# A graph layer with attention, linear mixing and a mixture of experts: the mixing product moved beside the edge gathers, the node stage unrolled, expert choice and placing rearranged

## The reference, cut to what matters

```python
xn = layernorm(x)
# graph attention, 4 heads of 64
h = (xn @ W).reshape(n, 4, 64)
logits = leaky_relu(a_src[src] + a_dst[dst], 0.2)
alpha = softmax of logits over the edges of one dst
gnn = relu(segment_sum(alpha * h[src], dst) + bias)
# linear attention, 4 heads of 32: one context matrix for all nodes
k = softmax(xn @ W_k, over the nodes);  context = k^T v;  mix = (q*scale) @ context @ W_out + b_out
x = x + gnn + mix
# mixture of experts, 8 experts, the best 2 of each node
xf = layernorm(x);  gate = xf @ Wg + bg;  top 2, softmax over the two
x = x + sum_e w_e * (gelu(xf @ W1[e] + b1[e]) @ W2[e] + b2[e])
```

## Time and profile before

| what | us |
|---|---|
| median of 3 runs | 1132.69 |
| lowest, highest | 1130.98, 1139.04 |
| the profiled execution | 1128.08 |
| its span | 1126.2 |
| TensorE busy | 935.8 (83%) |
| DVE busy | 514.0 (46%) |
| ACT busy | 364.9 (32%) |
| POOL busy | 596.7 (53%) |

### The profile page before, as it was taken

One profiled execution on the slowest core, in us unless ns is written; L12 is line 12 of the kernel. 1 busy time (PEld: TensorE's weight loads), 2 busy tenths in 40 slices (PEclk: granted clock), 3 DMA queues, 4 the chain that ended last, 5 costly groups with the idle time before them and its releaser, 6 DMA issues. The chain is left out here.

```text
span 1126.2 us, 19443 instructions
## 1 busy us (share of the span) xinstructions
PE 935.8 (83%) x5146; PEld 809.9 (72%) x5147; DVE 514.0 (46%) x1398; ACT 364.9 (32%) x1055; POOL 596.7 (53%) x591
## 2 busy tenths in 40 slices
PE   4999878878777687787864955699999999999995
PEld 3897656657566575665743845699999999899994
DVE  5488665665665656656646767111111111111110
ACT  4754332323323323333211310233333333333331
POOL 2477777777777777777739006233333333333331
PEclk9998787786878868778686867899999999999998
DMA  6356655555555555555684310466655666656561
GB/s 199 101 151 191 167 162 160 156 162 156 159 162 155 161 162 155 162 160 157 166 271 148 133 63 1 170 186 185 181 170 172 179 184 186 184 157 179 180 187 20
DMA packets 84353, 178.40 MB, mean 158 GB/s; under 512 B 12351, under 2 KB 41707, under 8 KB 84193
## 3 DMA queue, kind: packets, MB, share of 16 engines
q1 hardware_dynamic: 52449, 107.16, 28.6%
q0 software_dynamic: 30336, 69.57, 25.3%
q10 hardware_dynamic: 1536, 1.31, 0.5%
HBM read 160.76 MB, written 17.23 MB: 158 GB/s over the span
## 5 line engine op out<-in xcount | busy, mean ns | idle before, releaser
L405 POOL DMA_INDIRECT gathered<-h_table,src_row x416 | 393.9, 947 | 130.8 <-issue 128.4
L646 PE MATMUL bank<-gathered,one_hot 128*128 128x260 f32 x832 | 291.7, 512 | 2.9 <-DVE gathered L836 2.9
L635 PEld LDWEIGHTS bank<-adc,w_sb 128*128 128x128 f32 x832 | 128.2, 231 | 144.5 <-issue 140.4
L646 PEld LDWEIGHTS bank<-gathered,one_hot 128*128 128x128 f32 x832 | 200.9, 253 | 40.8 <-issue 3.7
L1426 POOL DMA_INDIRECT out<-y,add_index x54 | 85.7, 1587 | 249.9 <-DVE read_index L1516 124.8
L635 PE MATMUL bank<-adc,w_sb 128*128 x832 | 129.2, 283 | 101.7 <-ACT w_sb L506 101.2
L1483 PEld LDWEIGHTS bank<-xgT,w_slot 128*128 128x128 f32 x1728 | 202.7, 193 | 3.2 <-issue 0.6
L1448 ACT ACTIVATE hiddenT<-bank,b_slot 128x128 f32<-128x128 f32 x432 | 123.1, 368 | 249.6 <-PE bank L1483 249.5
L1483 PE MATMUL bank<-xgT,w_slot 128*128 128x128 f32 x1728 | 203.0, 276 | 0.2 <-DMA w_slot<-in_L_ffn_W 0.2
L1501 PE MATMUL bank<-w_sb,hiddenT 128*128 x864 | 196.5, 381 | 0.0
L1501 PEld LDWEIGHTS bank<-w_sb,hiddenT 128*128 128x128 f32 x864 | 160.2, 190 | 20.8 <-issue 0.4
(11 more groups left out here) (225 smaller groups left out, 674.7 us busy)
## 6 DMA issues: line engine op xcount, KB each, us to landing
w_slot<-in_L_ffn_W SPq DMA_DIRECT2D x54, 1024.0 KB, 6.0
w_sb<-key_table SPq DMA_DIRECT2D x104, 256.0 KB, 3.4
w_sb<-in_L_ffn_W SPq DMA_DIRECT2D x8, 1024.0 KB, 13.2
gathered<-h_table,src_row POOLq DMA_INDIRECT x416, 3.0
h_table<-acc SPq DMA_DIRECT2D x25, 130.0 KB, 1.9
xn_table<-xn SPq DMA_DIRECT2D x5, 640.0 KB, 3.3
out<-xs SPq DMA_DIRECT2D x4, 640.0 KB
xs<-in_x SPq DMA_DIRECT2D x3, 640.0 KB, 11.7
```

Source lines behind the costliest of these rows:

```text
L405: pool.indirect_dma_start(gathered[:, r, j, :], None, h_table, bass.IndirectOffsetOnAxis(ap=src_row[:, t:t + 1], axis=0)).then_inc(gather_ ...
L635: mm = pe.matmul(ad_bank[r % ADS][:, j * 2 * HEADS:(j + 1) * 2 * HEADS], one_hotT[:, r % 2, j, :], flat(adc[:, bass.ds(k, 1), :]), start=T ...
L646: mm = pe.matmul(sum_bank[r % SUMS][:, 0:ROW], one_hot[:, r, j, :], gathered[:, r, j, :], start=(j == 0), stop=(j == G - 1))
```

## The change

- **Front.** DVE instead of ACT copies h from PSUM, and adds the attention bias to it (zeros to the two attention columns). DVE's other work of the front is dealt out in small portions behind the copies of tiles 0 to 20 (`beside`). The bias load comes one place earlier in ACT's DMA list and is waited for with the weights.
- **Edge stage.** The first 64 groups instead of 8 are straight code on SP, ACT, TensorE and DVE. `w_mix` is made in groups 3 to 9: TensorE puts its products behind those of `spread`, in a free part of the same bank, ACT copies them out between its exponentials. From group 12 on, every second group carries the mixing product of one tile (TensorE) and its addition to `xs` (DVE), written to `x_mixed`, in memory that later holds the second-layer weights of experts 0 to 3. The context is scaled and masked by DVE ahead of group 0. SP's six weight loads at the end are gone.
- **Node stage.** Rounds of 2, 3, 5, 5, 5, 3 and 2 tiles, all straight code. No mixing, no bias addition. ACT normalises (scale and shift), DVE keeps inverse root and shift. Two halves of `xn` and of `xnT_slot`: round i waits for the store of round i - 2. SP loads the second-layer weights of experts 4 to 7 ahead of the stores and of 0 to 3 behind them, then the first-layer weights of the first two tiles as soon as the tiles' experts are known.
- **Search.** Both choices are made for all 25 tiles at once: maximum, comparison, rank of the first hit. The scans run on `choice` itself; TensorE adds the running counts by a second product into the same bank, with a triangle of -1.
- **Placing.** Four buffers instead of two; ACT multiplies by the shares, POOL by the node numbers; the tiles' experts are worked out after the fourth round.

The diff, cut:

```diff
+STATIC = 8 * RING
+MIX_FROM, MIX_STEP = 12, 2
+POSTS = ((0, 2), (2, 5), (5, 10), (10, 15), (15, 20), (20, 23), (23, 25))
 KGRP = -(-NT // G)
+PLACES = 4
...
-                for r in range(RING):
-                    step(c * NGRP + r, r, r, RING)
-                with eng.Fori(1, NGRP // RING - 1) as i:
+                for s in range(STATIC):
+                    step(c * NGRP + s, s, s % RING, RING)
+                with eng.Fori(STATIC // RING, NGRP // RING - 1) as i:
...
-                    sp.wait_ge(ctx_taken, 1)
-                    sp.wait_ge(x_biased, len(LOADS))
-                    for e in range(NX - 2):
-                        sp.dma_start(w2_sb[:, e * KF:(e + 1) * KF, :],
-                                     w2[e:e + 1, :, :].rearrange("e (k p) d -> p (e k) d", p=P)).then_inc(w2_in, 16)
...
+                        copies = {3: (w_qT, w_qT_ready), 4: (ctxT, ctxT_ready), 6: (ctx_out, ctx_out_ready),
+                                  8: (w_mix[:, 0, :], w_mix_ready), 9: (w_mix[:, 1, :], w_mix_ready)}
+                        if isinstance(s, int) and s in copies:
+                            copy, ready = copies[s]
+                            act.activation(copy, spare_of(r)[:, 0:copy.shape[-1]], ACT.Copy).then_inc(ready, 1)
...
+                    def chain(c, s, last):
+                        aside = spare_of(s)
+                        if s == 3:
+                            for k in range(KD):
+                                last = pe.transpose(aside[:, k * P:(k + 1) * P], w_q[:, k, :], ident[:, :])
+                        if s == 4:
+                            pe.wait_ge(ctx_ready, 1)
+                            last = pe.transpose(aside[:, 0:P], ctx, ident[:, :])
+                        if s == 6:
+                            pe.wait_ge(ctxT_ready, c + 1)
+                            last = pe.matmul(aside, ctxT, w_o, start=True, stop=True)
+                        if s in (8, 9):
+                            pe.wait_ge(ctx_out_ready, c + 1)
+                            pe.wait_ge(w_qT_ready, c + 1)
+                            last = pe.matmul(aside, w_qT[:, (s - 8) * P:(s - 7) * P], ctx_out, start=True, stop=True)
+                        t = mixed_tile(s)
+                        if t is not None:
+                            if t == 0:
+                                pe.wait_ge(w_mix_ready, c * 2 + 2)
+                            for k in range(KD):
+                                last = pe.matmul(aside, xnT[:, t, k * P:(k + 1) * P], w_mix[:, k, :], start=(k == 0), stop=(k == KD - 1))
+                        return last
...
+                    for t in range(NT):
+                        dve.wait_ge(projected, t + 1)
+                        dve.tensor_tensor(acc[:, t, :], bank[2 + t % 2][:, 0:D + 2 * HEADS], gat_bias_sb[:, :], ALU.add).then_inc(h_copied, 1)
+                        beside(t)
...
+                        t = mixed_tile(s + 2)
+                        if t is not None:
+                            dve.tensor_tensor(x_mixed[:, t, :], xs[:, t, :], spare_of(r + 2), ALU.add)
...
+                            after_one(dve.reciprocal(key_sum, bank[5][:, HID:HID + 1]))
+                            dve.tensor_scalar(ctx, bank[5][:, 0:HID], key_sum, QSCALE, ALU.mult, ALU.mult).then_inc(ctx_taken, 1)
+                            dve.wait_ge(ctx_taken, 1)
+                            dve.wait_ge(pool_ready, 7)
+                            dve.wait_ge(x_biased, len(LOADS))
+                            dve.tensor_tensor(ctx, ctx, head_mask[:, :], ALU.mult).then_inc(ctx_ready, 1)
...
+                    for e in range(NX // 2, NX):
+                        second_layer(e)
                     sp.wait_ge(zeros_ready, 1)
                     sp.dma_start(out[N:N + SPARE, :], zeros[:, :]).then_inc(out_started, 16)
-                    for i in range(NR):
-                        tiles = slice(i * UNROLL, min((i + 1) * UNROLL, NT - 1))
+                    for i, (low, high) in enumerate(POSTS):
                         sp.wait_ge(x_step, i + 1)
-                        sp.dma_start(out[tiles.start * P:tiles.stop * P, :].rearrange("(t p) d -> p t d", p=P),
-                                     xs[:, tiles, :]).then_inc(out_started, 16)
-
-                        sp.wait_ge(xn2_ready, (i + 1) * UNROLL)
-                        sp.dma_start(xn_table[i * UNROLL * P:(i + 1) * UNROLL * P, :].rearrange("(t p) d -> p t d", p=P),
-                                     xn[:, :, :]).then_inc(xn_stored, 16)
+                        stop = min(high, NT - 1)
+                        sp.dma_start(out[low * P:stop * P, :].rearrange("(t p) d -> p t d", p=P),
+                                     xs[:, low:stop, :]).then_inc(out_started, 16)
+                        sp.wait_ge(xn2_ready, high)
+                        sp.dma_start(xn_table[low * P:high * P, :].rearrange("(t p) d -> p t d", p=P),
+                                     xn[:, half(i):half(i) + high - low, :]).then_inc(xn_stored[i % 2], 16)
+                    for e in range(NX // 2):
+                        second_layer(e)
                     sp.dma_start(out[(NT - 1) * P:N, :], xs[0:LAST, NT - 1, :]).then_inc(out_started, 16)
-                    sp.wait_ge(xn_stored, 16 * NR)
-                    sp.wait_ge(out_started, 16 * (NR + 2))
+                    sp.wait_ge(experts_ready, 1)
+                    for u in range(2):
+                        sp.dma_start(w1_slot[:, u, :, :], first_layer(sp, u)).then_inc(w1_in[u], 16)
...
+                    for low, high in POSTS:
+                        sums = acc[:, low:high, 0:D].rearrange("p t (h c) -> p t h c", c=C)
+                        pool.tensor_tensor(sums, sums, rden[:, low:high, :].unsqueeze(3).broadcast_to((P, high - low, HEADS, C)),
                                            ALU.mult).then_inc(gat_scaled, 1)
...
+                        act.wait_ge(moments2_ready, high)
+                        act.activation(rstd[:, low:high], moments[:, low:high, 1], ACT.Sqrt, bias=eps_col[:, :]).then_inc(std2_ready, 1)
+                        act.wait_ge(shift2_ready, i + 1)
+                        if i >= 2:
+                            act.wait_ge(turned2, banks_upto(i - 1))
+                            act.wait_ge(xn_stored[i % 2], 16 * (i // 2))
+                        for t in range(low, high):
+                            act.activation(xn[:, half(i) + t - low, :], xs[:, t, :], ACT.Identity, bias=shift_col[:, t:t + 1],
+                                           scale=rstd[:, t:t + 1]).then_inc(xn2_ready, 1)
+                        if i >= 2:
+                            act.wait_ge(gated, POSTS[i - 2][1])
...
+                    for m in range(NCHOICE // UNROLL):
+                        act.wait_ge(tiles_found, m + 1)
+                        for k in range(UNROLL):
+                            n = m * UNROLL + k
+                            op = act.activation(what[m % PLACES][:, k, 1, :], in_tile[m % PLACES][:, k, :], ACT.Copy,
+                                                scale=share[:, n // NT, n % NT:n % NT + 1])
+                        op.then_inc(shares_ready, 1)
...
+                    pe.matmul(bank[0][:, 0:NCHOICE * NX], not_before[:, :], flat_choice, start=True, stop=False)
+                    pe.wait_ge(upto_ready, 1)
+                    pe.matmul(bank[1][:, 0:NX], ones[:, :], upto_count[:, NCHOICE - 1, :], start=True, stop=True).then_inc(totalled, 1)
+                    pe.matmul(bank[0][:, 0:NCHOICE * NX], ones[:, :], upto_count.rearrange("p n e -> p (n e)"),
+                              start=False, stop=True).then_inc(counted, 1)
...
+                    def invert(i):
+                        low, high = POSTS[i]
+                        dve.wait_ge(std2_ready, i + 1)
+                        dve.reciprocal(rstd[:, low:high], rstd[:, low:high]).then_inc(rstd2_ready, 1)
+                        dve.wait_ge(rstd2_ready, i + 1)
+                        dve.scalar_tensor_tensor(out=shift_col[:, low:high], in0=moments[:, low:high, 0], scalar=-1.0,
+                                                 in1=rstd[:, low:high], op0=ALU.mult, op1=ALU.mult).then_inc(shift2_ready, 1)
...
+                    def choose(k):
+                        after(dve.tensor_reduce(best[:, k, :], gate[:, :, :], AX.X, ALU.max))
+                        after(dve.tensor_tensor(ranked[:, :, :], gate[:, :, :], best[:, k, :].unsqueeze(2).broadcast_to(each), ALU.is_equal))
+                        after(dve.tensor_tensor(ranked[:, :, :], ranked[:, :, :], by_rank, ALU.mult))
+                        after(dve.tensor_reduce(first_rank[:, k, :], ranked[:, :, :], AX.X, ALU.max))
+                        after(dve.tensor_tensor(choice[:, k * NT:(k + 1) * NT, :], by_rank,
+                                                first_rank[:, k, :].unsqueeze(2).broadcast_to(each), ALU.is_equal))
+                    choose(0)
```

(9 more changed lines are left out.)

535 lines of the change are left out of this document (239 added, 296 removed).

## The result

The changed kernel took **1096.42 us** (median of 4 runs, 1091.57 to 1097.33) beside 1134.18 us before (4 runs, 1130.98 to 1139.04): ratio 0.9655, 95% interval 0.9608 to 0.9701. Forecast were 1090 us and 1076 to 1107. So the two profiles differ by 30.8 us, the medians by 37.8.

A forecast was written before the change was run, and what follows sets the result against it. POOL's gathers were taken to bound the edge stage (520 us) and TensorE the expert tiles. Terms summed to -41.3 us: 1128.1 becomes 1086.8, or 1091.4 from 1132.7, stated as 1090 us, range 1076 to 1107.

The forecast's parts named there:

- rivals C: Edge stage: mixing isn't hidden and lengthens the edges by 30 us of TensorE; about 1130 us, chance 0.03.
- D: Edge stage: unrolled straight code can't be supplied at the gathers' pace; at 6.1 us a step 1153 us, chance 0.03.
- Front: the failed term: Front, up to the first gather: copies and bias additions moved to DVE cost +1 us, bounds -2.5 and +4.
- The lock between POOL and the scalings: Front: DVE scalings and POOL's b_o additions can block each other; five scalings took 10.69 us in the node stage, 1.7 otherwise.
- Tail: End of the edges: without W2 loads the last logits and what follows come 3.9 us earlier, bounds -4.5 to 0.
- Node stage: Node stage: without mixing and bias additions it ends at 636 against 660.9, -25 us, bounds -37 to -20.
- The queue of the stores: Node stage: round 0's store waits behind W2 loads on SP's queue, so round 2 starts at about 609 instead of 598.
- rival A: Node stage: round 2's wait is short, giving 9 us more, at full clock another 3; 1078 to 1082 us, chance 0.2.
- The half clock: Node stage: TensorE at half clock makes five tiles take 6.6 us instead of 5.4, ending at 637 rather than 632.
- rival B: Front, placing, node stage, first tile: gains come half, through blocking, half clock and small w1 cover; 1105 us, chance 0.2.
- Choice and slots, placing: Routing: batched maxima and searches -1.5 us, running count -4 us; placing rounds at 1.7 us each, -4.6 us.
- First gather and W1: First expert tile: with w1 loaded during the placing, its gather lands in about 3.4 us instead of 6.1, -2.7 us.

The follow-up runs named there:

- before_again: The kernel before the change, run again unchanged on a chip where gathers land late: 1265.71 us.
- after_again: The changed kernel, run again unchanged on a chip where gathers land late: 1228.37 us, ratio 0.9701 to the kernel before.
- Experiment 1: Changed kernel with VectorE's front list reordered, averages, roots and shifts earlier: ratio 0.9642 to the kernel before.
- experiment 5: Kernel before, with only its six W2 loads moved from the end of the edges to behind the node stage's stores: ratio 1.0017.
- e10_wide: Changed kernel with VectorE's front list reordered, W2 loads behind the stores, and one extra 128x256 product per node-stage tile: 1087.82 us, ratio 0.9589.
- experiment 3: Changed kernel with the four W2 loads ahead of the node stage's stores issued behind them: ratio 0.9667 to the kernel before.
- experiment 8: Changed kernel with POOL making both products of each placing round and ACT none: ratio 0.9778 to the kernel before.
- experiment 6: Changed kernel with the first two W1 loads issued in the expert stage again instead of during the placing: ratio 0.9751 to the kernel before.

## Why the prediction was right, and where it was not

**Where the time went** was right: node stage, routing and first gather gave 39.4 us, and the edges gave and cost nothing (rivals C and D fall with the first pair of profiles, and again with `before_again` and `after_again`).

**Front: the failed term.** I put +1 and bounded it at +4; it was +5.0 on both chips, outside the bounds. The step that failed was adding up VectorE's work (1.3 us a tile, "and 1.1, TensorE's pace, for the rest") as if its order didn't matter. What cost was that averages, roots and shifts stood behind additions which themselves wait for TensorE, which waits for ACT, which waits for the shift. Experiment 1 leaves all the work in place and gets 51.8 us, so the load was not the limit. The lock between POOL and the scalings was seen and named, and is real (1.23 against 0.17 us), but is by its length the smaller part; experiment 1 undid both at once.

**Tail: 1.6 of 3.9 us.** The logits came 3.0 us earlier, 0.9 less than reckoned; the slowest gather had landed after 6.9 us, now after 4.6. That fits the W2 loads, but isn't shown by a run: experiment 5 found nothing of it on a late chip. Then the last two sums took 5.46 us instead of 4.06 and gave 1.4 back, and 6.71 in `e10_wide`, where the whole tail was 15.3 us, as long as before. The stretches around these sums, before and then after:

```profile
580.00:584.00 4.00, 1.18 (x5) 1.06 (x6) 3.40 (x7) 0.32 (x2) 0.00 (x0) 1.00 1.10 347
584.00:588.00 4.00, 2.85 (x12) 1.82 (x10) 2.41 (x5) 0.00 (x0) 0.00 (x0) 1.00 0.11 37
```

```profile
581.00:585.00 4.00, 0.55 (x2) 0.49 (x3) 3.14 (x8) 0.32 (x2) 0.00 (x0) 0.97 0.00 0
585.00:589.00 4.00, 4.00 (x13) 3.21 (x12) 2.11 (x4) 0.00 (x0) 0.00 (x0) 0.61 0.00 0
```

Before, late gathers had left TensorE 16 products to catch up at 574, it stood idle for 2.87 us ahead of the last sums and ran them at a clock of 1.00. Now it has caught up earlier, stands idle for 3.85 us, and the clock falls to 0.61 in the sums. The forecast moved everything behind the logits by 3.9 us and left TensorE's clock out of it. That the sums are longer because the clock is lower is read from these three traces; no run held it up there. What lowers it isn't shown: in `e10_wide` 16 products ran until 574.9, the idle time was 3.10 us, little more than before, and the sums had a clock of 0.50. In eight profiles from late chips the idle time was 1.2 us and these sums took 4.05 or 4.06 us.

**Node stage: right by two errors, which is luck.** The queue of the stores was there, but it cost 3.0 us (experiment 3), not the 9 of rival A: without it round 2 starts 18.2 us into the stage instead of 21.3, and no earlier, since DVE and POOL block each other in the first rounds (L1283 takes 2.37 us for 1280 elements where it takes 1.46 later; L1278, 2.09 us for two columns, 0.17 later). I had round 2 start 9.8 us into the stage and 11 later for the queue with its small stores; it was 18.2 and 3.1. So 8.4 us too few stood against 7.9 too many. That the lead is the lock of DVE and POOL is read from these rows; no run took POOL's scaling out. The half clock, which I gave 6.6 us a round, held for the whole stage at 6.3. I had priced the lock at nothing in the central value and at 5 in rival B. From the start of round 2 to the end I forecast 27.9 us, and it took 28.2. The Trainium skill, page TensorE: Matmul & The Clock Gate, section HAM oscillation, blames idle gaps between bursts for a low clock. Here the gaps don't explain it: with none in the profile the clock stayed at 0.50 (30 instructions in 6.00 us), and it rose when wide products were put between the others.

**Choice and slots, placing.** -6.3 against -5.5 and -6.1 against -4.6. The mechanism held, the size was off: DVE and POOL do alternate, but at 1.56 us a round, where I had 1.7, and 1.9 for strictly in turn. By the rows of the round above it is 0.81 for L1358 (to 665.29), 0.5 from there to the end of POOL's product (665.80) and 0.3 to the end of the next L1356, with which L1358 overlaps by 0.1. I had put in 0.82, 0.65 and 0.45. The page SBUF — State Buffer of the Trainium skill, section Who interferes with whom, says that a VectorE instruction with two SBUF inputs and a reading GpSimd instruction exclude each other; experiment 8 agrees: one more POOL product, and DVE's L1357 takes 1.18 us, where the same line took 0.81.

**First gather and W1:** -3.1 against -2.7, shown by experiment 6 (2.5). **Expert tiles:** forecast 0; the +5.8 in the profiles is of the size by which executions differ, so 0 stands. **Mixing:** the term was 0 and is 0, but of the 29.6 us that I added to TensorE's busy time in the edges only 3.0 came, at a clock of 0.82 instead of 0.78. So the cover had less to take than I said.

In the medians 37.8 of the 41.3 us came. By the stages 4.9 us are missing: the front's 4.0, the tail's 2.3 and the node stage's 1.8, less the 2.4 that the routing gave beyond its terms and 0.8 of first gather and edges. That would leave 36.4; the other 1.4 are within what executions differ by.

## What to carry to other kernels

When work is given to an engine that already feeds the others, add up the order and not only the load: ask of each of its results who waits for it, and put it ahead of any instruction that waits for that same chain. A wait that a profile will show is worth only what isn't waited for anyway: look for the second-latest arrival before pricing it. Price a stretch of small products on TensorE at both of its clock levels, also where it will have no idle time.
